# Attention block with FP4 feed-forward: the output projection from float32r halves, made by GpSimd during the attention

## The reference, cut to what matters

```
q, k, v = (split_heads(einsum(x, w) * s + b) for each of q, k, v)   # 16 heads of 16
ctx  = softmax(q k^T / 4) v                                          # per head, S = 1024
x1   = layernorm(x + (einsum(ctx, w_o) * s_o + b_o))                 # the output projection
gate, up = fp4(x1) @ fp4(w_gate)^T, fp4(x1) @ fp4(w_up)^T            # width 704
out  = layernorm(x1 + fp4(silu(gate) * up) @ fp4(w_down)^T)
```

## Time and profile before

| | |
|---|---|
| median of 3 runs | 1953.62 us (1952.57 to 1954.31) |
| the profiled execution | 1955.24 us, its span 1953.4 us |
| PE busy | 1922.9 us, 98% |
| DVE busy | 1828.6 us, 94% |
| ACT busy | 1641.7 us, 84% |
| POOL busy | 918.3 us, 47% |
| DMA moved | 181.47 MB, mean 93 GB/s |

### The profile page before, as it was taken

The page is one execution under the profiler, slowest core; times in us unless marked ns, Lnnn a source line. Parts: engine busy times, 40 slices in busy tenths (PEclk is TensorE's granted clock), DMA queues, the critical chain, the costliest instruction groups (busy, mean ns, idle before and its releaser), DMA issues.

```text
span 1953.4 us, 43156 instructions
## 1 busy us (share of the span) xinstructions
PE 1922.9 (98%) x15934; PEld 1112.8 (57%) x15934; DVE 1828.6 (94%) x3087; ACT 1641.7 (84%) x3225; POOL 918.3 (47%) x779
## 2 busy tenths in 40 slices
PE   8999999999999999999999999999999999999998
PEld 7776444444444444444444444444478888888876
DVE  4799999999999999999999999998299999999997
ACT  6655999999999999999999999998867777777776
POOL 3000446675776665365122122212156666666785
PEclk9999999999999999999999999999999999999999
DMA  7985633444354445435434543542111111111200
GB/s 225 303 262 211 116 56 47 84 89 106 77 106 90 90 94 100 95 78 103 96 85 94 101 95 78 103 96 85 40 36 49 49 50 49 49 50 55 66 30 28
DMA packets 127199, 181.47 MB, mean 93 GB/s; under 512 B 37836, under 2 KB 82636, under 8 KB 126988
## 3 DMA queue, kind: packets, MB, share of 16 engines
q1 hardware_dynamic: 119308, 171.10, 36.8%
q10 hardware_dynamic: 7392, 7.34, 1.2%
q0 software_dynamic: 288, 0.27, 0.1%
HBM read 103.68 MB, written 73.40 MB: 91 GB/s over the span
## 4 chain that ended last, share of the span: by engine, by line
DVE 63%; PE 33%; issue 2%; ACT 1%; DMA 0%; DVEq 0%; SPq 0%; POOLq 0%; POOL 0%; ACTq 0%
DVE halfmax L1154 43%; DVE halfmax L1149 14%; PE ps L1430 10%; PE ps L1469 6%; PE ps L505 4%; PE ps L517 2%; PE ps L1418 2%; PE ps L1441 2%; PE ps L1064 2%; PE ps L1030 1%; PE ps L492 1%; PE ps L1477 1%; DVE room L1620 1%; PE ps L476 1%; PE ps L1486 1%
## 5 line engine op out<-in xcount | busy, mean ns | idle before, releaser
L1115 ACT ACTIVATE room<-ps 128x512 f32<-128x512 f32 x2048 | 1086.1, 599 | 106.4 <-PE ps L1030 80.4
L1154 DVE TENSOR_REDUCE halfmax<-ps 128x1 f32<-128x512 f32 x1470 | 901.2, 678 | 0.0
L1030 PE MATMUL ps<-qs,ks 50*128 50x512 f32 x2048 | 718.9, 449 | 2.6 <-DVE halfmax L1154 1.2
L1005 PE MATMUL ps<-ks,qs 48*128 48x512 f32 x1960 | 678.7, 439 | 4.8
L1064 PE MATMUL ps<-room,vals 128*17 128x256 f32 (+2 forms) x8192 | 578.7, 384 | 0.2 <-ACT craw L1123 0.2
L1005 PEld LDWEIGHTS ps<-ks,qs 48*128 48x128 f32 x1960 | 311.4, 184 | 407.0 <-DVE halfmax L1154 250.0
L1030 PEld LDWEIGHTS ps<-qs,ks 50*128 50x128 f32 x2048 | 325.1, 184 | 19.9 <-ACT room L1115 14.1
L1064 PEld LDWEIGHTS ps<-room,vals 128*17 128x17 f32 x8192 | 167.5, 96 | 251.4 <-issue 187.9
L1149 DVE TENSOR_REDUCE halfmax<-ps 128x2 f32<-128x1024 f32 x245 | 296.3, 1209 | 0.9 <-PE ps L1005 0.8
L164 POOL CAST mrow<-turned_rows 128x32 fp32r<-128x32 f32 x32 | 6.7, 210 | 576.0 <-DVE turned_rows L159 576.0
L1430 PE MATMUL ps<-wguT,xqT 128*128 128x512 f32 (+1 forms) x1152 | 266.8, 384 | 3.9 <-DVE xqT L1660 3.9
(11 more groups left out here) (120 smaller groups left out, 2266.6 us busy)
## 6 DMA issues: line engine op xcount, KB each, us to landing
qk_parts<-parts SPq DMA_DIRECT2D x64, 512.0 KB, 5.4
qs<-qk_parts SPq DMA_DIRECT2D x192, 128.0 KB, 4.3
ks<-qk_parts SPq DMA_DIRECT2D x192, 128.0 KB, 6.7
ctx_raw<-craw SPq DMA_DIRECT2D x64, 256.0 KB
ready<-passing SPq DMA_DIRECT2D x27, 512.0 KB, 4.8
pairs<-ready SPq DMA_DIRECT2D x27, 512.0 KB
out_dram<-fin SPq DMA_DIRECT2D x64, 128.0 KB, 1.9
xin<-in_L_attn_x_dram ACTq DMA_DIRECT2D x14, 512.0 KB, 6.8
```

Of the source, the lines that this page charges most:

```text
L1005: nc.tensor.matmul(ps[:, MX + max_number(i, u, bank) % 4, :], qs[rows, i.slot(RING), pair, t * P:(t + 1) * P], ks[rows, i.slot(RING), pair ...
L1030: nc.tensor.matmul(ps[:, score_bank(i, s, n), :], ks[rows, slot, pair, kt * P:(kt + 1) * P], qs[rows, slot, pair, qh * BANK:(qh + 1) * BAN ...
L1115: nc.scalar.activation(prob[:, prob_slot(i, s), score_order(i, s)[n], :], ps[:, score_bank(i, s, n), :], ACT.Exp, scale=float(D) ** -0.5). ...
L1154: nc.vector.tensor_reduce(halfmax[:, i.slot(2), bank, column:column + 1], ps[:, at + bank, :], AX.X, ALU.max, negate=True).then_inc(max_re ...
```

## The change

The output projection of the 54 tiles that come ready from the attention is done as three float32r products (high by high, high by low, low by high) instead of one float32 product. For this w_o is kept in two halves (`wo_half`), made in `project`; the float32 copy stays for the last 10 tiles. GpSimd makes the context's two halves in `pass_pair`: one cast and one subtraction of 128x512 elements, after the additions that were there. SP stores the halves (512 KB, as before) and, by a second DMA, x plus b_o (256 KB), and `load_passing` waits for both stores. `feed` loads a pair by two DMAs. The raw context of the last 10 tiles goes to two other buffers, `passing` and `late`, loaded one step pair later than before.

```diff
         def copy_weights(m):
             act.wait_ge(wT_psum, m + 1)
+            if m == 3:
+                nc.scalar.activation(wT[:, :, :], ps[:, w_bank(m), :].rearrange("p (c o) -> p c o", c=HC), ACT.Copy)
...
+            if i.k == 1:
+                split_weights(3)
...
-            wait(sp, passing_stored, 16 * p)
-            load_raw(sp, p, x_tok, ctx_dram, rden_dram, passing, passing_in)
+            wait(sp, passing_stored, 32 * p)
+            load_raw(sp, p, ctx_dram, rden_dram, passing[:, 0], passing[:, 2], passing_in)
+            load_x(sp, p, x_tok, passing[:, 1], passing_in)
 
         def store_passing(p):
-            sp.wait_ge(passing_ready, 2 * (p + 1))
-            sp.dma_start(ready_dram[p].rearrange("p (a c n) -> p a c n", a=2, c=HC), passing[:, 0:2]
+            sp.wait_ge(passing_ready, 4 * (p + 1))
+            sp.dma_start(ready_dram[p].rearrange("p (a c n) -> p a c n", a=2, c=HC), passing_half[:, :].bitcast(F32)
                          ).then_inc(passing_stored, 16)
+            sp.dma_start(plus_dram[p].rearrange("p (j h) -> p j h", j=2), passing[:, 1]).then_inc(passing_stored, 16)
...
             last.then_inc(passing_ready, 1)
+            pool.wait_ge(passing_ready, 4 * p + 1)
+            wait(pool, passing_stored, 32 * p)
+            nc.gpsimd.tensor_copy(passing_half[:, 0], passing[:, 0]).then_inc(passing_ready, 1)
+            pool.wait_ge(passing_ready, 4 * p + 3)
+            nc.gpsimd.tensor_tensor(passing_half[:, 1], passing[:, 0], passing_half[:, 0].bitcast(F32),
+                                    ALU.subtract).then_inc(passing_ready, 1)
...
+        def load_late(p):
+            if p == READY:
+                sp.wait_ge(passing_stored, 32 * READY)
+                for qh in range(QH):
+                    sp.wait_ge(craw_stored[qh], 32 * NGR)
+                sp.wait_ge(rden_stored, 16 * QH * NGR)
+            if p >= READY + 2:
+                sp.wait_ge(sems["wo_psum"], 2 * p - 2)
+            load_raw(sp, p, ctx_dram, rden_dram, *raws[p % 2], raw_in[p % 2])
...
             for c in cs:
-                last = nc.tensor.matmul(ps[:, WO, 0:H], pairs[:, pair % PAIRS, 0, c, half * P:(half + 1) * P], wT[:, 1, c, :],
-                                        start=c == 0, stop=c == HC - 1)
+                if t.k >= RAW:
+                    last = nc.tensor.matmul(ps[:, WO, 0:H], raws[pair % 2][0][:, c, tokens], wT[:, c, :],
+                                            start=c == 0, stop=c == HC - 1)
+                    continue
+                for n, (a, b) in enumerate(PRODUCTS):
+                    last = nc.tensor.matmul(ps[:, WO, 0:H], pairs[:, pair % PAIRS, a, c, tokens], wo_half[:, b, c, :],
+                                            start=n == 0 and c == 0, stop=n == len(PRODUCTS) - 1 and c == HC - 1)
```

More of the change, by code:

```diff
@@ L244, in build @@
         passing = sb("passing", [P, 3, HC, 2 * P])
-        pairs = sb("pairs", [P, PAIRS, 3, HC, 2 * P])
+        pairs = sb("pairs", [P, PAIRS, 2, HC, 2 * P], F32R)
+        plus = sb("plus", [P, PAIRS, 2, H])
         wguT = sb("wguT", [P, 2, HC, 2 * I], F32R)
@@ L252, in build @@
         spare = sb("spare", [P, 1])
+        passing_half = sb("passing_half", [P, 2, HC, 2 * P], F32R)
+        late = sb("late", [P, 2, HC, 2 * P])
+        raws = ((passing[:, 0], passing[:, 2]), (late[:, 0], late[:, 1]))
+        raw_in = [sem(f"raw_in{j}") for j in range(2)]
         third = feed(nc, sem, room, fq, buffers, x_tok, ctx_dram, rden_dram, out_tok, ps, ident, wT, s_all, b_row,
                      wguT, wd, wdT, wt_psum, wt_ready, wt_split, numbers, sums, craw_ready, craw_stored, rden_ready, rden_stored,
-                     ready_dram, pairs, pair_in, passing_stored)
+                     ready_dram, plus_dram, pairs, plus, raws, raw_in, pair_in, passing_stored, wo_half)
         with ExitStack() as inner:
@@ L292, in _, with project @@
                 third.vector(dve, range(FILL, TILES_RUN))
-def project(nc, sb, sem, x_tok, ws, ss, bs, ffn_ws, amax_w, rcp_w, scales_done, qk_dram, vals, ps, ident, wT, s_all, b_col, b_row, numbers, weights_in,
+def project(nc, sb, sem, x_tok, ws, ss, bs, ffn_ws, amax_w, rcp_w, scales_done, qk_dram, vals, ps, ident, wT, wo_half, s_all, b_col, b_row, numbers, weights_in,
             qk_consts_in, vo_consts_in, qs, ks, stack_in, negmax, halfmax, maxima_out, qk_stored, qk_float, v_ready):
@@ L632, in split_weights @@
             dve.wait_ge(wT_ready, m + 1)
-            high, low = (wqk[:, part, m] if m < 2 else wv[:, part] for part in range(2))
+            high, low = (wqk[:, part, m] if m < 2 else (wv, wo_half)[m - 2][:, part] for part in range(2))
             nc.vector.tensor_tensor(low, ps[:, w_bank(m), :].rearrange("p (c o) -> p c o", c=HC),
@@ L1384, in sync @@
                 load(t)
+            if i.k % 2 == 0 and READY <= i.k // 2 + 1 and i.plus(2).ok(NT):
+                load_late(i.k // 2 + 1)
             t = i.plus(-9)
@@ L1655, in vector @@
                 nc.vector.scalar_tensor_tensor(out=y[:, :], in0=ps[:, WO, 0:H], scalar=s_all[:, 3:4],
-                                               in1=pairs[:, pair % PAIRS, 1, half], op0=ALU.mult,
+                                               in1=plus[:, pair % PAIRS, half], op0=ALU.mult,
                                                op1=ALU.add).then_inc(sems["wo_used"], 1)
@@ L1731, in gpsimd @@
                 pool.wait_ge(pair_in[pair % PAIRS], pair_loads(pair))
-                raw, rcp = (pairs[:, pair % PAIRS, part, :, half * P:(half + 1) * P] for part in (0, 2))
+                pool.wait_ge(raw_in[pair % 2], 64 * ((pair - READY) // 2 + 1))
+                raw, rcp = (part[:, :, half * P:(half + 1) * P] for part in raws[pair % 2])
                 nc.gpsimd.tensor_tensor(raw, raw, rcp, ALU.mult).then_inc(sems["ctx_ready"], 1)
-                with_b = pairs[:, pair % PAIRS, 1, half]
+                with_b = plus[:, pair % PAIRS, half]
                 nc.gpsimd.tensor_tensor(with_b, with_b, b_row[:, 1], ALU.add).then_inc(sems["xb_ready"], 1)
```

47 lines of the change are left out of this document (24 added, 23 removed).

## The result

| | before | changed |
|---|---|---|
| median | 1953.8 us (1951.32 to 1954.31, 6 runs) | 1965.39 us (1963.91 to 1969.08, 6 runs) |
| ratio | | 1.0066, 95% interval 1.0053 to 1.0079 |
| the profiled execution | 1955.24 us | 1966.14 us, span 1964.3 |

A forecast was written before the change was run, and what follows sets the result against it. The prediction took VectorE to bound the attention and TensorE to be busy throughout the feed stage. Profiled 1955.24 plus 15.8 lost in the attention, feed stage nothing, gave 1971.0; the median, 1.6 lower, 1969.4 us, range 1953.0 to 1983.0.

The forecast's parts named there:

- The ring: Attention: the round through GpSimd, SP and the buffer passing is only 1.0 us in 265 shorter than the attention itself.
- The added 2.8 us a round: Attention: subtraction 1.28, cast 0.6, waits 0.16 and second store 0.8 lengthen each round by 2.8 us, between 1.65 and 4.15.
- the 0.44 that the prediction weighed: GpSimd's cast in the attention: 0.44 us by a reference page's rule, against the 0.6 us that the forecast took.
- the 4.1 us of room: Attention: lateness absorbed before a load falls behind L164, from its 3.08 us lead and the ring's 1.0 us.
- What is free: Attention: a load may come 2.5 us after its L164 without loss, 3.1 at most, 0.1 at least.
- 18.3 - 2.5 = 15.8: Attention: the load comes 18.3 us late against L164, 2.5 are free, so 15.8 us are lost, between 6.0 and 29.0.
- The feed stage at nothing: Feed stage: the shorter projection gains nothing, since the transposes wait for ScalarE; 8.9 us as the other bound.
- the loop through VectorE: Feed stage: a loop of VectorE, ScalarE and TensorE's transposes sets the period, 16.40 us for two tiles.
- The price of 0.19 us a tile: Feed stage: projection takes 0.70 us instead of 0.89, saving TensorE 0.19 us a tile.
- The signs: Profile: some attention groups of 40 to 42 us, maxima's DMAs 6 us or more after L164, two tiles in 16.4 us.
- Loss and gain: Rival: the attention's loss comes and the feed stage gains 8.9 us, 1960.5 us in all; chance 0.13.
- GpSimd slows VectorE: Rival: new GpSimd work lengthens VectorE's maxima in the attention, 19 us more, so 1988 us; chance 0.04.

The follow-up runs named there:

- experiment 3: Kernel before plus GpSimd's cast and subtraction and the second store, float32 projection kept: 1966.98 us against 1952.14 for the kernel before.
- experiment 4: The change with five GpSimd weight operations between two groups' maxima instead of six: 1952.01 us against 1953.52 for the kernel before.
- experiment 5: Kernel before with five GpSimd weight operations between two groups' maxima instead of six, as a control: 1953.95 us against 1953.59.
- experiment 8: The change with pass_pair and its store as before, six float32r products on the unsplit context: 1951.52 us against 1952.14 for the kernel before.
- experiment 1: Kernel before plus GpSimd's cast and subtraction into an unread buffer, store and projection as before: 1961.17 us against 1952.14.
- experiment 2: Kernel before plus only a second store of x plus b_o (256 KB), which load_passing also waits for: 1953.87 us against 1952.14.
- experiment 9: The kernel of experiment 8 with two products a tile instead of six: 1950.87 us against 1953.52 for the kernel before.
- experiment 10: Kernel before with two ScalarE feed-stage operations (square of h, addition behind it) on 352 of 704 columns: 1952.18 us against 1953.59.
- experiment 11: The change with five weight operations and the same two ScalarE operations on half the columns: 1950.74 us, ratio 0.9983 to the kernel before.
- experiment 6: The change with a second buffer for passing, so a load waits for the store of two pairs before: 1961.96 us against 1953.52 for the kernel before.
- experiment 7: The change with the maxima's eight DMAs ahead of load_passing in SP's list: 2002.78 us against 1953.52 for the kernel before.
- experiment 12: The change with five weight operations, ScalarE's square of h and addition moved behind h's transpose copy: 2189.59 us against 1953.59 for the kernel before.

## Why the prediction came out as it did

The forecast was 1969.4 us, its own range 1959.6 to 1982.6; measured were 1965.39. The mechanism, the place and the sign were right. By its steps:

- **The ring.** That rounds of `passing` were only 1.0 us in 265 shorter than the groups was right, and experiments 3, 4, 5 and 8 show it from both sides: with the two edits the loss is there without the float32r projection; without them, or with one weight operation less, it isn't.
- **The added 2.8 us a round.** The subtraction took 1.28 and the cast 0.61 us, as forecast (not the 0.44 that the prediction weighed). The seven rounds grew from 37.8 to 40.3 us, so by 2.5, and the one ahead of them by 3.0 (365.79 to 407.75, against 38.94 us before). In the terms of the sum: the load of 690.03 is 1.55 us behind its L164, and its group had lost 15.1 us by then, so it is 16.6 us late where I had 18.3; with the 4.1 us of room that is 20.7 in eight rounds, 2.6 each. The two operations alone gave 1.9 and the second store alone 0.9 by the same count.
- **What is free.** I gave 2.5 us of lateness for nothing; this term was mis-sized. In the change a load 0.89 us after L164 cost nothing, and those at 1.31 and 1.55 cost 1.4 and 0.7 us. In experiments 1 and 3 loads at 2.26, 2.95 and 2.32 cost 1.40, 2.17 and 1.14. So about 1 us was free. Those of the change at 2.38, 3.49 and 4.84 cost 3.04, 4.65 and 6.0, more than their lateness less 1, and in each of these groups TensorE's clock fell; so it did in experiment 2 (2.59 late, 2.7 lost) and in the last long group of experiment 1 (2.54 late, 3.2 lost). The forecast's argument had no term for that.
- **Two errors that cancel.** 18.3 - 2.5 = 15.8 was forecast; 16.6 - 0.85 = 15.75 was measured, with the 0.85 that was free in the last late group. That the two came out alike is luck: the rounds grew less than I had, and less was free.
- **The feed stage at nothing.** Nearly right: 1.6 us, which experiments 4 and 5 confirm (-1.5 and nothing). The step that the earlier trace rows shows waits for ScalarE's copy, and I took both steps to be so. In the other one the float32 projection held the transposes 0.10 us longer than the copy did. With that gone nothing more is to be had from a shorter projection (experiment 9). That the loop through VectorE sets the period alone was not right: a loop of TensorE's gate and ScalarE's L1571 to L1580 closes at the same length (experiments 10 and 11). The price of 0.19 us a tile is neither confirmed nor refuted, since the transposes wait for ScalarE in both steps; the six weight loads took 0.77 and not 0.70 us.
- **Not in the sum.** The profiled execution was forecast at 1971.0 us and took 1966.14. Of these 4.9 us, 1.6 are the feed stage's, and 2.6 come from a fall of the clock that the profiled execution of the kernel before had near the attention's end and that of the change had not. The second differs from one execution to the next.
- **The signs.** Five groups of 39.3 to 43.9 us came where 40 to 42 were named, with the waits that were named; the maxima's DMAs were issued 5.4 to 7.9 us after L164 in the three longest. Two tiles took 16.3 us, not 16.4.
- **The rivals.** Loss and gain both came, but the gain is 1.6 and not 8.9 us. "GpSimd slows VectorE" is excluded by experiment 4.

## What to carry to other kernels

An engine that is idle for a third of the time can still have no room, when what it feeds comes back to it through a queue of DMAs: follow one buffer for a whole round, from load to load, and compare the round with the period. A wait on a landing is worth the idle time that it shows, not the duration of the landing. And before pricing a faster piece on the busiest engine, look whether the next instruction behind it already starts on another engine's signal.

## What the runs showed of the hardware that I had not expected

TensorE's granted clock fell to the lower of its two levels, 1.2 GHz (0.50), behind three of the stalls: for 3.4 us from about 537 and from about 578, and for 6.8 us from about 657. Windows of the changed kernel round the last of them:

```profile
652.00:656.00 4.00, 2.51 (x27) 1.11 (x23) 3.05 (x6) 2.34 (x5) 0.00 (x0) 1.00 0.52 155
656.00:660.00 4.00, 2.11 (x13) 1.11 (x17) 1.25 (x2) 1.22 (x3) 3.58 (x5) 0.61 0.04 6
660.00:664.00 4.00, 4.00 (x32) 1.40 (x26) 2.50 (x3) 1.98 (x5) 3.91 (x3) 0.54 0.00 0
664.00:668.00 4.00, 4.00 (x44) 2.02 (x46) 3.67 (x7) 3.75 (x8) 3.92 (x2) 1.00 0.50 138
```

TensorE was busy for 2.5 of the 4.8 us ahead of the fall, and then worked at half the clock; VectorE, which waits for it, is busy for 1.25 and 2.5 us of the next two stretches of 4. The three groups with such a fall are the three with the largest excess (4.65, 3.04 and 6.0 us). Loads of nearly the same lateness tell what the fall adds: 2.38 us late with a fall of 3.4 us cost 3.04, while 2.26 and 2.32 late without one cost 1.40 and 1.14 (experiments 1 and 3). So such a fall adds some 1.6 us to the wait that came before it.

The same is seen away from any late load. From ScalarE's copy of a context half at 1351.27 to the next at 1374.15 the kernel before takes 22.88 us, with a fall of 6.8 us from about 1357. The same stretch takes 21.5 us in experiments 2, 4 and 5, with a fall of 3.4 us in each, and 20.3 us in the change and in experiments 1, 3 and 6 to 12, without one. Experiment 10 has the attention of the kernel before, unchanged, and is among these last. So the 2.6 us that seemed to come back at the attention's end differ from one execution to the next and are no effect of the change. Whole runs agree: of the 27 runs of the kernel before that stand beside experiments 5, 10 and 11, the ten with a mean granted clock of 0.997 take 1954.9 us on the mean and the nine with 0.999 take 1952.7. Differences of one or two us between medians, as in experiments 4 and 8 to 11, have to be read with this in mind; the length of two tiles in the trace is the safer number.
